# Induced phase: second uses of two norms moved from VectorE to ScalarE as scale and shift

## The reference

```python
def _ln(x, g, b):
    mu = jnp.mean(x, axis=-1, keepdims=True)
    var = jnp.var(x, axis=-1, keepdims=True)
    return (x - mu) / jnp.sqrt(var + 1e-05) * g + b

def _mab(q, k, v, p):
    in_w, in_b, out_w, out_b, g1, b1, g2, b2, l1w, l1b, l2w, l2b = p
    x = q + _mha(_ln(q, g1, b1), _ln(k, g1, b1), _ln(v, g1, b1), in_w, in_b, out_w, out_b)
    h = _ln(x, g2, b2)
    ff = jax.nn.gelu(h @ l1w.T + l1b, approximate=False) @ l2w.T + l2b
    return x + ff

h = tower(...)                                   # (8, 512, 128)
x = _layernorm(h)                                # no gain, no bias
h = h + _mab(x, _mab(ind, x, x, p1), _mab(ind, x, x, p1), p2)
h = h + ffn(_layernorm(h))                       # group gate on this norm; a second norm inside for the inner gates
```

## Time and profile before

| what | us |
|---|---|
| median of 3 runs | 2388.35 (2387.33 to 2389.3) |
| profiled execution, its time | 2404.56 |
| its span | 2402.7 |
| PE busy in the span | 2019.5 (84%) |
| DVE busy | 1340.1 (56%) |
| ACT busy | 1156.6 (48%) |
| POOL busy | 778.4 (32%) |

### The profile page before, as it was taken

The page is one execution under the profiler, slowest core; times in us unless marked ns, Lnnn a source line. Parts: engine busy times, 40 slices in busy tenths (PEclk is TensorE's granted clock), DMA queues, the critical chain, the costliest instruction groups (busy, mean ns, idle before and its releaser), DMA issues. The chain is left out here.

```text
span 2402.7 us, 44240 instructions
## 1 busy us (share of the span) xinstructions
PE 2019.5 (84%) x14601; PEld 1445.8 (60%) x14601; DVE 1340.1 (56%) x4495; ACT 1156.6 (48%) x2495; POOL 778.4 (32%) x975
## 2 busy tenths in 40 slices
PE   5799999999999999999998367887676329999986
PEld 4466666666566666666565245554443219999972
DVE  2365556555665656555663246777566505555547
ACT  2476666665666666656663024544433204443434
POOL 0012222122222222122222111234566725555546
PEclk7799999999999999999998667787866559999995
DMA  3641334123432344124300233452121157777754
GB/s 99 123 73 26 54 67 67 38 31 67 68 55 50 55 67 67 40 29 67 67 1 1 79 74 81 78 93 44 44 50 39 55 171 243 230 227 217 212 151 146
DMA packets 113988, 207.11 MB, mean 86 GB/s; under 512 B 23076, under 2 KB 47654, under 8 KB 113112
## 3 DMA queue, kind: packets, MB, share of 16 engines
q1 hardware_dynamic: 102616, 184.90, 34.3%
q0 software_dynamic: 10176, 17.09, 2.2%
q10 hardware_dynamic: 976, 2.30, 0.4%
HBM read 147.59 MB, written 64.66 MB: 88 GB/s over the span
## 5 line engine op out<-in xcount | busy, mean ns | idle before, releaser
L679 ACT ACTIVATE tower_prob<-tower_prob,tower_negmax 128x386 f32<-128x386 f32 (+1 forms) x768 | 390.5, 556 | 303.4 <-DVE tower_negmax L886 302.7
L886 DVE CUSTOM_DVE_ANT_0 tower_prob<-tower_sbank,tower_band 128x386 f32<-128x386 f32 (+1 forms) x768 | 346.2, 488 | 141.5 <-PE tower_sbank L453 136.2
L491 PEld LDWEIGHTS tower_tbank<-tower_ident,tower_prob 128*128 128x128 f32 x1920 | 228.2, 143 | 129.5 <-issue 81.7
L491 PE MATMUL tower_tbank<-tower_ident,tower_prob 128*128 128x128 f32 x1920 | 284.8, 279 | 22.1 <-DVE tower_probT L911 20.4
L735 ACT ACTIVATE tower_probT<-tower_tbank 128x384 f32<-128x384 f32 (+1 forms) x576 | 227.6, 430 | 127.4 <-PE tower_tbank L491 125.3
L2052 POOL DMA_INDIRECT scratch_yt<-experts_y,experts_rows x190 | 186.7, 983 | 185.1 <-DVE experts_y L2195 117.0
L430 PE MATMUL tower_dbank<-tower_oxT,tower_w 96*128 96x512 f32 x384 | 191.5, 624 | 13.9 <-ACT tower_oxT L724 13.9
L2110 PE MATMUL experts_ybank<-experts_w,experts_hid 128*128 128x128 f32 x1520 | 185.1, 275 | 0.0
L2098 PE MATMUL experts_hbank<-experts_zT,experts_w 128*128 128x256 f32 x760 | 183.7, 385 | 1.1 <-ACT experts_zT L2134 1.1
L453 PE MATMUL tower_sbank<-tower_k_st,tower_q_st 49*128 49x386 f32 (+1 forms) x768 | 161.2, 414 | 25.7 <-POOL tower_k_st L635 14.3
L2143 ACT ACTIVATE experts_hid<-experts_hbank,experts_w 128x256 f32<-128x256 f32 x190 | 79.7, 470 | 202.9 <-PE experts_hbank L2098 147.8
(11 more groups left out here) (314 smaller groups left out, 3447.2 us busy)
## 6 DMA issues: line engine op xcount, KB each, us to landing
experts_w<-ew SPq DMA_DIRECT2D x95, 578.0 KB
scratch_qk<-tower_qk SPq DMA_DIRECT2D x64, 384.0 KB, 4.6
tower_q_st<-scratch_qk SPq DMA_DIRECT2D x96, 192.0 KB, 7.8
tower_k_st<-scratch_qk SPq DMA_DIRECT2D x96, 192.0 KB, 10.7
experts_rows<-scratch_zs SPq DMA_DIRECT2D x95, 132.0 KB
scratch_kq<-induce_kq SPq DMA_DIRECT2D x8, 1024.0 KB, 4.3
experts_res<-scratch_yt SPq DMA_DIRECT2D x8, 1024.0 KB, 6.8
induce_k_st<-scratch_kq SPq DMA_DIRECT2D x48, 128.0 KB, 4.3
```

The costliest lines, as they stand in the source:

```text
L491: mm = pe.transpose(bank[:, jb * P:jb * P + P], prob[:, hg % PR, at + jb * P:at + jb * P + P], ident[:, :])
L679: act.activation(prob[:, hg % PR, 0:width(i)], prob[:, hg % PR, 0:width(i)], ACT.Exp, bias=negmax[:, hg % PR:hg % PR + 1], scale=-1.0).the ...
L886: scores.copied(dve.tensor_tensor_reduce(prob[:, hg % PR, 0:width(i)], bank[:, 0:width(i)], band[:, BAND_AT[i]:BAND_AT[i] + width(i)], sca ...
```

## The change

`twice` on POOL also computes a shift, -mean x factor, for the two norms of kinds `HEAD` and `FF2`: one wait for its own power and two small instructions with a wait between them. ACT gets `centre`, which applies factor and shift as scale and bias of an Identity activation, four an item. `x2` and `x5` are made there, at the same steps `X2` and `X5_NORM`, at the end of ACT's pieces for that item. DVE's two `normalise` calls for them are gone; those for `x3` and `zn` stay.

```diff
             def twice(kind, m):
                 pool.wait_ge(moments, stat_order[kind, m])
                 k = slot_of(kind, m)
...
                 pool.tensor_tensor(both, both, half[:, :], ALU.pow).then_inc(roots, 1)
+                pool.wait_ge(roots, stat_order[kind, m])
+                ch.mark(pool.tensor_tensor(shift[:, k, :], mv[:, k, :, 0], rstd[:, k, 0, :], ALU.mult))
+                ch.after()
+                pool.tensor_scalar(shift[:, k, :], shift[:, k, :], -1.0, None, ALU.mult).then_inc(shifts, 1)
...
+            def centre(k, m, dst, src, sem):
+                act.wait_ge(shifts, shift_order[k, m])
+                k = slot_of(k, m)
+                for t in range(NT):
+                    ins = affine(dst[:, t, :], src[:, t, :], rstd[:, k, 0, t:t + 1], shift[:, k, t:t + 1])
+                ins.then_inc(sem, 1)
...
+                if p == X2:
+                    if m:
+                        dense.wait_copied(act, ("y2", m - 1))
+                    centre(HEAD, m, x2, h[m % NH], x2_ready)
+                if p == X5_NORM:
+                    if m:
+                        dense.take(act, ("x5T", m - 1))
+                        act.wait_ge(base_ready, m)
+                    centre(FF2, m, x5, h2, x5_ready)
...
-                if p == X2:
-                    normalise(HEAD, m, x2, h[m % NH], x2_ready)
...
-                if p == X5_NORM:
-                    if m:
-                        dense.take(dve, ("x5T", m - 1))
-                        dve.wait_ge(base_ready, m)
-                    normalise(FF2, m, x5, h2, x5_ready)
```

More of the change, by code:

```diff
@@ L1005, in induce @@
         st6, mv = ph.sb("st6", [P, LNS, NT, 6]), ph.sb("mv", [P, LNS, NT, 2])
-        rstd = ph.sb("rstd", [P, LNS, 2, NT])
+        rstd, shift = ph.sb("rstd", [P, LNS, 2, NT]), ph.sb("shift", [P, LNS, NT])
         scores = Ring(ph, [ph.psum(f"sbank{j}") for j in range(2)], "s_")
@@ L1015, in induce @@
         consts_set, scaled, ones_in, o_clear = (ph.sem(n) for n in ("consts_set", "scaled", "ones_in", "o_clear"))
-        moments, roots, normed = ph.sem("moments"), ph.sem("roots"), ph.sem("normed")
+        moments, roots, normed, shifts = (ph.sem(n) for n in ("moments", "roots", "normed", "shifts"))
         x2_ready, x2b_ready, y1b_ready, x5_ready = (
@@ L1062, in items @@
             return [(m, g - m * PERIOD) for m in range(B) if A_STAT <= g - m * PERIOD <= SCATTER[-1]]
-        exp_order, stat_order, norm_order = {}, {(IND, 0): 1}, {(IND, 0): 1}
+        exp_order, stat_order, norm_order, shift_order = {}, {(IND, 0): 1}, {(IND, 0): 1}, {}
         STATS = {A_STAT: FINAL, A_MOM: HEAD, Y1: ATT1, DOWN1: FF1, Y2_MOM: ATT2, DOWN2: FF2}
         NORMS = {A_NORM: FINAL, A_X3: HEAD, Y1_NORM: ATT1, R1_NORM: FF1, Y2_NORM: ATT2, Z_NORM: FF2}
+        SHIFTS = {A_MOM: HEAD, DOWN2: FF2}
         for g in STEPS:
             for m, p in items(g):
-                for numbers, at in ((stat_order, STATS), (norm_order, NORMS)):
+                for numbers, at in ((stat_order, STATS), (norm_order, NORMS), (shift_order, SHIFTS)):
                     if p in at:
@@ L1415, in root, with twice @@
                 pool.tensor_tensor(rstd[:, k, 0, 0:n], rstd[:, k, 0, 0:n], half[:, 0:n], ALU.pow).then_inc(roots, 1)
-            def twice(k, m):
-                pool.wait_ge(moments, stat_order[k, m])
-                k = slot_of(k, m)
+            def twice(kind, m):
+                pool.wait_ge(moments, stat_order[kind, m])
+                k = slot_of(kind, m)
                 pool.tensor_scalar(rstd[:, k, 0, :], mv[:, k, :, 1], EPS, None, ALU.add)
```

## The result

The changed kernel takes 2402.76 us, the median of 7 runs (2397.97 to 2406.35), beside 2387.33 us for the kernel before (7 runs, 2384.63 to 2395.4). The ratio is 1.0061, 95% interval 1.0047 to 1.0075: 14.6 us slower (11 to 18), where +5.0 was forecast. The time lies outside the range of 2387 to 2400.

A forecast was written before the change was run, and what follows sets the result against it. No engine alone was taken as the bound, but a chain hopping between PE, DVE, POOL and ACT. The terms 4.2 + 1.3 + 8.7 - 6.2 - 3.0 = +5.0 us gave 2393.4 us, range 2387 to 2400.

The forecast's parts named there:

- What bounds the kernel: Induced phase: a chain hopping between engines sets the end; the phase's end hangs on the last choice, POOL's length covered.
- POOL's pair: Two shift instructions ahead of POOL's `root`, in 7 periods at 0.6 us: +4.2 us, bounds 3.5 and 9.8.
- Rival C: POOL's pair is blocked in every period, 1.4 us instead of 0.6 in 7 places: +10.6 us, 2399.0; chance 0.16.
- `HEAD`'s pair: Shift pair after `HEAD`'s power, and after the last item's `FF2` power, meets DVE work: +1.3 us, bounds 0 and 4.
- `x5` on ACT: PE stalls for `x5`, which ACT makes behind two exponentials, at items 0 to 6: +8.7 us.
- `x2` off DVE: DVE's choice starts sooner without `x2` of items 2 to 7, 6 x 1.03: -6.2 us.
- Meetings: Later DVE chains lose less to the port shared with POOL, five meetings at 0.6 us: -3.0 us, bounds 0 and -7.5.
- rival B: DVE-POOL meetings decide, port term -7.5: +0.5 us, 2388.9; against it, POOL's bias would catch a later instruction; chance 0.22.
- Rival D: Exponentials come early enough that ACT's `x5` is ready when PE asks, +8.7 unpaid: -5.0 us, 2383.4; chance 0.10.
- What would show it: Profile signs: `root` 0.7 us after the power, `yn` waits 45 us, seven `x5` waits, choice waits some 1 us shorter.
- three signs of being wrong: PE's wait for `x5` missing, POOL's pair costing over 1 us, or DVE's choice instructions no longer stretched.

The follow-up runs named there:

- pool_tail: The kernel before with five unused POOL powers added behind the phase's last scatter; 8.1 us slower than before (ratio 1.0034).
- shift_only: The changed kernel with `x2` and `x5` both given back to DVE, POOL's shifts computed but unread; +7.6 us (4 to 11) against before.
- x2_only: The changed kernel with `x5` given back to DVE and its POOL pair dropped, only `x2` on ACT; -6.7 us (-10 to -4) against before.
- c_before: The kernel before, unchanged, run again for a second profile; 2388.68 us.
- filler: The changed kernel with PE making the transposes of `zn` three times ahead of its wait for `x5`; +1.7 us (-1 to 5) against before.
- x5_only: The changed kernel with `x2` given back to DVE and its POOL pair dropped, only `x5` on ACT; +32 us (28 to 36) against before.
- x5_first: The changed kernel with ACT's `x5` moved ahead of the exponentials of its step; 7.2 us faster than before (ratio 0.9970).
- late_shift: The changed kernel with POOL's pair moved behind all roots of its step; +7.9 us (5 to 11) against before.

## Why the prediction was wrong, point by point

- **What bounds the kernel.** The loop was right: the edits on it moved the time. The reading of its end was wrong. "POOL's own length is covered there" rested on the 16.73 us of the earlier trace rows, one execution's padding. With 3.2 us instead, and `pool_tail` paying 8.1 us for 8.54, POOL's scatters of the last items end the phase. By the argument of the prediction it costs the sum little, since a delayed choice counts at either end.
- **POOL's pair, +4.2 (bounds 3.5 and 9.8).** Right: waits for `yn` 45.4 us against 41.3, and +3.8 in `shift_only`. By time `shift_only` measured 7.6 with `HEAD`'s pair in it, for which the two terms had 5.5, inside the bounds. Rival C, with 9.8 for the pair, falls on the profile: the pair takes 0.69 us with its gaps, not 1.4. That C's +10.6 came nearest of all rivals to the 14.6 is luck.
- **`HEAD`'s pair, +1.3.** Not seen apart from the rest. `x2_only`, which has that pair, waits for `yn` as long as `c_before` (41.2 us) and shows nothing of it from add to gates (-0.3).
- **`x5` on ACT, +8.7.** This step failed, and by omission. The stall itself was right: 9.9 us, less the 1.7 to 1.9 that PE had waited for DVE's `x5` before, is 8.0 to 8.2, and at item 0 it is 1.71 against 1.90. (Item by item it was less so: items 3 and 4 stalled for 1.61 and 0.90 us where the sum had 0.78 and 0.33, and "DVE's `x5` was done by the time PE had transposed `zn`" was not so at items 2 and 4.) What stands behind the stall was priced at nothing, as if PE would work on at its old speed. The stretch from add to gates grew 22.7 us in after. Less 3.8 for the pair and 8.2 for the stall, 10.7 are left, and `filler`, in which the clock is back, takes 9.7 off at items 0 to 3, where `c_before` had it (14.2 in all). So the half clock is worth some 10 us there. Behind the gates `x5_only` has 4.5 more, no clearer than the 4.0 between two profiles of one kernel. The term should have stood at 17 (`x5_only`, 20.8 less the pair's 3.8) to 21 (with that 4.5), not 8.7. A hint was in the rows: the earlier trace rows show the same four transposes at 1.11 us at item 3 and at 0.60 at item 0, so at item 0 PE had full speed to lose. What they could not show is that item 3 had it too in the second profile (1.00).
- **`x2` off DVE, -6.2.** Right in sum: -6.7 by time, -6.7 on its stretch in `x2_only`. That it comes so close is part luck: the six places of 1.03 each measured from -2.7 to +1.1, and the clock in them differed from `c_before`'s by up to 0.14. Beside `x5` on ACT it is worth 8.4 by the stretches (-3.9 against +4.5), and 17 by the times (14.6 against 32), which isn't explained. The sign it was to be known by is blurred: PE's five waits for the choice are 21.2 us in after and 21.5 in the earlier trace rows, but 24.3 in `c_before`.
- **Meetings, -3.0.** Not shown. The choice of item 3 lost one: L1725's counterpart takes 0.32, but L1921 of the same chain now takes 1.69 beside POOL's bias, as rival B's "against" said, so the meeting moved instead of vanishing. PE waits there 3.52 us where it waited 4.60, about `x2`'s share. B falls.
- **Rival D, faster if ACT's `x5` is ready in time.** Its mechanism is what `x5_first` shows, at -7.2 us against the -5.0 worked out. "They can't come sooner" was true of the exponentials and beside the point: `x5` needs nothing of PE's in that step and could go ahead of them.
- **What would show it.** Its main signs came: `root` 0.69 us after the power, 45.4 us of waits for `yn`, seven waits for `x5` of 0.9 to 1.7 us. None of its three signs of being wrong came, and the time was out all the same: the list looked only for terms that were in the sum.

The rows on the choice of item 3 in the kernel after, timeline (against the earlier trace rows):

```profile
1775.03 1.69 DVE L1921 TENSOR_TENSOR induce_gs<-induce_gs 128x20 f32<-128x20 f32 x1
1775.40 1.27 POOL L1467 TENSOR_TENSOR induce_x<-induce_x,induce_erows 128x512 f32<-128x512 f32 x1
...
1777.34 0.45 PE L1299 MATMUL induce_dbank<-induce_chosen,induce_allones 128*128 128x128 bf16 x4 [3.52 <-DVE induce_chosen L1925]
```

With the term of `x5` at 17 to 21 and the meetings at 0 the sum is 4.2 + 1.3 + 17 - 6.2 = +16.3 to 4.2 + 1.3 + 21 - 6.2 = +20.3 on the loop. The stretches of after give 22.7 - 3.9 = +18.8, the next phase starts 17.2 us later, and the time is 14.6 (11 to 18).

## What to carry to other kernels

Where a change makes TensorE wait inside a stretch that runs at full clock, price the wait, and as a second case the stretch behind it at half speed; here the second was the larger (10.7 us against 8.2). When a block moves to another engine, look first at its place in that engine's queue: here the same block in ACT's idle time ahead of the exponentials turned +14.6 us into -7.2. And before a wait at a phase's end is taken as cover, or a clock as given, see it in a second execution.

## What the runs showed of the hardware

- **Behind a short stall of PE the clock was mostly at half.** Three kernels have the late `x5` (after, `x5_only`, `late_shift`). Of their 11 stalls of 0.9 to 1.7 us at items 0 to 3, 9 were followed by 0.50 to 0.53 around the gates and 2 by 0.90 and 1.00; at 4 of the 9 the transposes of `zn` ahead of the stall took 1.11 to 1.12 us, so there the clock was low already and did not come back. In the nine other profiles without added transposes 3 of 36 such windows had 0.50 and the rest 0.73 to 1.00, among them 0.92 to 1.00 behind nine waits of 0.4 to 1.1 us for DVE's `x5` at items 2 and 3. With transposes in part of the wait (`filler`) they ran at 0.73 to 1.00. What tips the clock at one item and not at another wasn't found. The Trainium skill, "TensorE: Matmul & The Clock Gate", section "What's actually happening", puts it that "the default state is throttled, and activity releases the throttle"; `filler` agrees.
- **The clock differs between executions of the same kernel.** In the first profile of before, item 3's gates ran at 0.50, in the second at 1.00, and its stretch was 3.18 us longer. Such stretches could account for the scatter of some 5 us from run to run; that wasn't tried. The window around item 3's gates in the first profile of before, beside the last of `c_before`'s four above:

```profile
1751.10:1758.60 7.50, 7.50 (x39) 6.25 (x42) 2.76 (x8) 2.43 (x5) 6.15 (x7) 0.50 0.64 129
```

- **ACT's price for scale and shift from two per-partition operands** was as the experts' rows gave it: 485 ns median, 1.64 us for four. The Trainium skill, "ScalarE: Activation LUTs", section "What ACT_TABLE_LOAD costs", gives 186 ns + 0.833 ns an element, 93 ns for each such operand and 93 ns of overlap: an estimate from it is 479 ns for one and 1.64 us for four. The runs agree.
